# Softmax coefficients sent to the partitions through DRAM, batches in even-first order, and a reordered start, in a two-block conditioned FFN kernel

## The chip, the cores and the metric

One core of a Trainium2 chip runs the whole program. The metric is the device time of one execution in microseconds; the profile is of one execution of the same program.

## The reference, cut to what matters

```python
# block 0: a mixture of 8 channel matrices per batch, then a linear layer with routed LoRA
h = gelu(cond @ W0 + b0); h = gelu(h @ W1 + b1)
att = softmax(h @ W2 + b2)                                  # (64 batches, 8)
agg_w = einsum('bk,koi->boi', att, weight); agg_b = att @ bias_k
z = einsum('boi,bih->boh', agg_w, x) + agg_b[:, :, None]    # channels mixed, per batch
x1 = x + (z @ Wf.T + routed LoRA of z)                      # gates: layer norm, relu, top 2 of 8
# block 1: a grouped convolution over positions, plus ctx = cond @ c_weight.T + fside, then FFN with 8 experts
out = x1 + ffn1(conv(x1) + ctx)
```

x is 64 batches by 64 channels by 1024. All is fp32; each large product is made of three products of rounded parts (high by high, high by low, low by high).

## The kernel before, in words

**Tiles.** The 4096 rows (batch, channel) are 32 tiles of 128 rows, two batches to a tile. Block 0 is phase A, block 1 is phase B. The mixing of channels and the linear layer commute, so phase A first multiplies each tile of x by the linear weights (`main(t, b, k)`, line 1409, in three banks of 384, 416 and 384 columns, 24 matmuls each) and then mixes the channels of that product with a 128x128 block-diagonal matrix of the tile (`mix(t, b, k)`, line 1429, three matmuls). Between the two, ACT rounds the product to a high part (`y_high`, line 746) and DVE writes the low part (`y_low`, line 985). DVE makes the mixing matrix of a tile (`mix_matrix`, line 962) from `attw`, the 8 channel matrices in `consts`, and `attc`, which holds on each partition the 8 softmax coefficients of each tile's batch (even batches on partitions 0 to 63, odd ones on 64 to 127). The bias of the mixture comes in through the column sums of the weights (`column_sums`, line 1379), scaled by `aggc`; `evict` (line 991) adds it and the residual and `route` (line 998) makes the gates.

**The start.** x and the weights of block 0 arrive as plain fp32. SP issues every DMA of the kernel (line 427 on), and the queue lands them in order: the first half of tile 0 of x (`xo`), the weight chunks 0 to 3 (one of the 8 row blocks of bank 0 each), the second half of tile 0 (line 460), chunks 4 to 7, the parameter pack `cbuf` (line 463), tile 1, tile 2, `consts`, chunks 8 and 9 (bank 1), 10 and 11 (bank 2). ACT makes the high part of each chunk (`split_hi`, line 724) and of each tile (`x_high`, line 739), DVE the low part (`split_lo`, line 957; `x_low`, line 979). PE warms up with 8 matmuls on constants and then runs `first_bank` (line 1390): bank 0 of tile 0 with its column sums, one row block after another as they come.

**The conditioning net** is done in between, on PE in five steps (`cond`, line 1357): 0, 1 and 2 are the three layers; 3 transposes `att`, makes the context product, and spreads `att` to the 128 partitions by a matmul of `batch_part` (which partition half a batch belongs to) with `att_m` (att times `batch_tile`, made by DVE at line 1054); 4 is the bias of the mixture. ACT does the GELUs (796, 799) and the exponential (802) with its table load (800), DVE the softmax (1050 to 1052) and the copy of the spread coefficients from PSUM to `attc` (1060). Batches lie in their natural order, so the two batches of a tile are neighbours.

**Order.** Each engine runs a list written out by hand, and semaphores join them; an engine does its list strictly in order. The orders that matter are PE at lines 1447 to 1476, ACT at 779 to 846, DVE at 1025 to 1129, SP at 457 to 493 and POOL at 675 to 694. After the start, PE repeats for each tile of phase A: main bank 1, mix of tile t + 2 bank 0, main bank 2, mix bank 1, main bank 0 of tile t + 3, mix bank 2.

## Time and profile before

| | |
|---|---|
| median of 3 runs | 1265.41 us (1264.41 to 1265.54) |
| the profiled execution's own time | 1265.09 us |
| its span, first to last instruction | 1263.3 us |
| granted TensorE clock, mean over the span | 1.000 |
| PE busy | 1257.2 us |
| DVE busy | 842.7 us |
| ACT busy | 307.3 us |
| POOL busy | 235.2 us |
| DMA moved | 141.55 MB, 112 GB/s in the mean |

The profile has one line for each group of instructions, with the engine, the kernel's line and the operation. PE is the matmul engine, DVE, ACT and POOL are the vector, scalar and general engines, and SP only issues DMAs. A timeline row gives the start from the span's beginning, the duration (of all its instructions together, where it says x2 or more), and in brackets how long the engine had been idle and what released it. Matmuls overlap on PE: the distance from one start to the next is what one costs. The chain of waits follows the work back from the end, at each step to what released it. All times are in microseconds.

### The profile page before, as it was taken

Reading aid. Unit: us, or ns where it says so; the run is one execution under the profiler, and the core shown is the slowest. Engines: PE = TensorE matmul, PEld = TensorE weight load, DVE = VectorE, ACT = ScalarE, POOL = GpSimd, SP = SyncE. Lnnn points to the kernel's source line nnn. Section 1 sums busy time; section 2 is a strip of 40 time slices with the busy share of each in tenths; the row PEclk is TensorE's granted clock in tenths of the full one; section 3 lists DMA queues with packets and bytes.
Section 4 is the critical chain, followed back from the end, with each engine's and each line's share of the span. In section 5 each row is a group of like instructions: output and inputs, shape, how many; then the busy total and the mean of one; then the engine's idle time right before and its main releaser. Section 6 shows DMA issues by size and latency. Waiting matters only on the chain.

```text
span 1263.3 us, 21216 instructions
## 1 busy us (share of the span) xinstructions
PE 1257.2 (100%) x6967; PEld 1165.1 (92%) x6967; DVE 842.7 (67%) x2171; ACT 307.3 (24%) x654; POOL 235.2 (19%) x170
## 2 busy tenths in 40 slices
PE   9999999999999999999999999999999999999998
PEld 8999999999999999888889889888888888988987
DVE  6877866667667667756765765675676576576563
ACT  6323332222223234211121121121121112112110
POOL 1244522232323222011001001001100100100100
PEclk9999999999999999999999999999999999999999
DMA  8355433333334267434223323322423322332310
GB/s 278 129 145 167 146 110 116 128 122 120 114 109 132 91 217 223 123 90 123 71 80 114 88 71 106 106 71 89 122 71 88 116 78 71 113 99 71 98 43 34
DMA packets 84889, 141.55 MB, mean 112 GB/s; under 512 B 6769, under 2 KB 53361, under 8 KB 84849
## 3 DMA queue, kind: packets, MB, share of 16 engines
q1 hardware_dynamic: 84848, 141.04, 36.7%
q8 instruction: 22, 0.36, 0.1%
q14 instruction: 19, 0.15, 0.0%
HBM read 88.57 MB, written 52.45 MB: 112 GB/s over the span
## 4 chain that ended last, share of the span: by engine, by line
PE 97%; DVE 1%; DMA 1%; ACT 0%; SPq 0%; issue 0%
PE ps L1345 30%; PE ps L1347 29%; PE ps L1346 29%; PE ps L1514 5%; PE ps L1516 2%; DMA xo<-in_xt 1%; DVE weights L960 1%; PE ps L1503 0%; PE ps L1480 0%; PE ps L1610 0%; DVE mixs L970 0%; PE ps L1505 0%; DVE mixw L969 0%; SPq L432 0%; ACT L800 0%
## 5 line engine op out<-in xcount | busy, mean ns | idle before, releaser
L1345 PE MATMUL ps<-weights,lhs_h 128*128 128x512 f32 (+3 forms) x1408 | 498.5, 354 | 0.0
L1347 PE MATMUL ps<-weights,lhs_l 128*128 128x512 f32 (+3 forms) x1408 | 489.1, 347 | 0.0
L1346 PE MATMUL ps<-weights,lhs_h 128*128 128x512 f32 (+3 forms) x1408 | 489.0, 347 | 0.0
L1345 PEld LDWEIGHTS ps<-weights,lhs_h 128*128 128x128 f32 x1408 | 264.5, 188 | 23.9 <-issue 0.6
L1347 PEld LDWEIGHTS ps<-weights,lhs_l 128*128 128x128 f32 x1408 | 264.5, 188 | 21.3
L1346 PEld LDWEIGHTS ps<-weights,lhs_h 128*128 128x128 f32 x1408 | 265.2, 188 | 19.8
L715 POOL TENSOR_TENSOR xo<-row,wsum 128x512 f32<-128x512 f32 x60 | 76.8, 1306 | 647.3 <-DMA out_x<-xo 647.3
L1345 PE MATMUL ps<-weights 128*128 128x384 f32 (+1 forms) x376 | 128.8, 343 | 0.0
L1346 PE MATMUL ps<-weights 128*128 128x384 f32 (+1 forms) x376 | 128.1, 341 | 0.0
L1347 PE MATMUL ps<-weights 128*128 128x384 f32 (+1 forms) x376 | 127.9, 340 | 0.0
L1231 DVE TENSOR_TENSOR whole<-ps,whole 64x256 f32<-64x256 f32 x240 | 101.2, 422 | 7.7
L752 ACT ACTIVATE part<-ps 128x384 fp32r<-128x384 f32 (+1 forms) x96 | 47.9, 499 | 239.9 <-PE ps L1347 239.9
L1224 DVE TENSOR_TENSOR whole<-ps,bias_in 64x256 f32<-64x256 f32 x240 | 101.1, 421 | 6.7 <-issue 0.2
L1514 PE MATMUL ps<-conv_hl,part 128*128 128x512 f32 x360 | 99.9, 345 | 0.0
L881 ACT ACTIVATE lhs_h<-whole 128x512 fp32r<-128x512 f32 x64 | 40.5, 633 | 235.6 <-DVE whole L1231 228.3
L988 DVE TENSOR_TENSOR part<-ps,part 128x384 fp32r<-128x384 f32 (+1 forms) x96 | 54.3, 565 | 61.0 <-ACT part L752 59.5
L668 POOL TENSOR_TENSOR row<-row,biased 128x800 f32<-128x800 f32 x31 | 61.2, 1974 | 127.3 <-DMA row<-in_xr 102.3
L1287 DVE TENSOR_TENSOR staging<-ps,mixw 128x256 f32<-128x256 f32 x32 | 13.6, 425 | 96.9 <-PE ps L1347 96.6
L1142 DVE TENSOR_TENSOR row<-ps,row 128x512 f32<-128x512 f32 x60 | 41.5, 692 | 52.8 <-PE ps L1347 52.5
L1514 PEld LDWEIGHTS ps<-conv_hl,part 128*128 128x128 f32 x360 | 67.7, 188 | 6.2
L1315 DVE TENSOR_TENSOR xo<-ps,xo 128x512 f32<-128x512 f32 x64 | 43.2, 692 | 45.3 <-PE ps L1347 45.1
L1347 PEld LDWEIGHTS ps<-weights 128*128 128x128 f32 x376 | 70.7, 188 | 0.4
(201 smaller groups left out, 1622.7 us busy)
## 6 DMA issues: line engine op xcount, KB each, us to landing
row<-spill SPq DMA_DIRECT2D x30, 576.0 KB, 4.2
z<-x_round SPq DMA_DIRECT2D x64, 256.0 KB, 5.1
out_x<-xo SPq DMA_DIRECT2D x31, 512.0 KB, 2.7
xo<-in_xt SPq DMA_DIRECT2D x30, 512.0 KB, 3.5
x_round<-row SPq DMA_DIRECT2D x60, 256.0 KB, 2.1
row<-in_xr SPq DMA_DIRECT2D x31, 400.0 KB, 3.2
spill<-row SPq DMA_DIRECT2D x31, 400.0 KB, 3.8
staging<-in_w SPq DMA_DIRECT2D x9, 832.0 KB, 6.1
```

The source lines that it names most:

```text
L668: pool.tensor_tensor(dst, dst, biased[:, BANK0:OUT0], ALU.add).then_inc(row_ready12, 1)
L715: pool.tensor_tensor(natural[:, PAD * (1 - h):PAD * (1 - h) + J // 2, :], src[:, q].rearrange("p (s i) -> p s i", i=P), b1bc[:, q].rearran ...
L752: act.activation(yh[:, slot, 0:COLS0[k]], ps[:, BY0[slot], 0:COLS0[k]], ACT.Copy).then_inc(y_hi[k], 1)
L988: dve.tensor_tensor(yl[:, slot, 0:n], ps[:, BY0[slot], 0:n], f32(yh[:, slot, 0:n]), ALU.subtract).then_inc(y_lo[k], 1)
L1142: dve.tensor_tensor(base[:, q], ps[:, BP0[h], :], base[:, q], ALU.add).then_inc(x1_ready, 1)
L1224: dve.tensor_tensor(where_to[to, b], parts[q, :, k, 0], add[to, b, :, None, :].to_broadcast([64, 2, J, GC]), ALU.add).then_inc(conv_part, 1)
L1231: dve.tensor_tensor(where_to[to, b], parts[q, :, k, 1], where_to[to, b], ALU.add).then_inc(conv_read, 1)
L1315: dve.tensor_tensor(o, ps[:, BQ[2 + h], :], o, ALU.add).then_inc(y_read, 1)
L1345: pe.matmul(out_ap, lhs[0], rhs[0], start=first, stop=False, skip_group_check=True)
L1346: pe.matmul(out_ap, lhs[0], rhs[1], start=False, stop=False, skip_group_check=True)
L1347: return pe.matmul(out_ap, lhs[1], rhs[0], start=False, stop=last, skip_group_check=True)
L1514: pe.matmul(dst[:, out_k], stationary(t, 0, h, g, w), both[:, rows], start=(w == 1), stop=False, skip_group_check=True)
```

## The change

The spread of the coefficients by DVE and PE is taken out. Instead SP writes `att` to DRAM (`att_rows`) and reads it back twice, once to each half of the partitions. For that the batches are laid out with the 32 even ones first and then the 32 odd ones, which the host does for `cond_128`, and the writing of the context rows (`cond_rows`, now two DMAs) and the bias pick on ACT follow. The parameter pack loses the two tables for the spread and has 594 columns in place of 754. Besides, the start is in another order: the second half of tile 0 is issued by ACT; steps 0 and 1 of the net are inside `first_bank`, step 2 ahead of tile 1, steps 3 and 4 a few row blocks earlier or later; ACT and DVE do the net's work ahead of the split of tile 2; `y_low(0, 0)` comes after the first mixing matrix; and for tile 0 `main(0, 0, 2)` comes ahead of `mix(2, 2, 0)`, with `y_high(0, 2)` and `y_low(0, 2)` earlier.

```diff
# DRAM tensors and the pack
-        cond_rows = nc.dram_tensor("cond_rows", (B, C), F32, kind="Internal").ap()
+        cond_rows = nc.dram_tensor("cond_rows", (TILES, 2, C), F32, kind="Internal").ap()
+        att_rows = nc.dram_tensor("att_rows", (2, TILES * KATT), F32, kind="Internal").ap()
-        CPACK = 754
+        CPACK = 594
# SP
             sp.dma_start(xo[:, 0, 0:512], a["xt"][0:P, 0:512]).then_inc(first_in, 16)
-            for n in range(4):
-                chunk(n)
-            sp.dma_start(xo[:, 0, 512:D], a["xt"][0:P, 512:D]).then_inc(xt_in[0], 16)
-            for n in range(4, 8):
+            for n in range(8):
                 chunk(n)
...
             chunk(8)
             chunk(9)
+            sp.wait_ge(cond_dve, 3)
+            sp.dma_start(att_rows.rearrange("h (t k) -> (h t) k", k=KATT), att).then_inc(att_out, 16)
             sp.wait_ge(x_lo, 3)
             chunk(10)
+            sp.wait_ge(att_out, 16)
+            for h in range(2):
+                sp.dma_start(attc[64 * h:64 * h + 64, :, :].rearrange("p t k -> p (t k)"),
+                             att_rows[h].unsqueeze(0).to_broadcast([C, TILES * KATT])).then_inc(attc_in, 16)
+            chunk(11)
             load_xr0(0, 0)
-            chunk(11)
...
-            sp.wait_ge(cond_dve, 6)
-            sp.dma_start(cond_rows, ctxo).then_inc(cond_out, 16)
+            sp.wait_ge(cond_dve, 5)
+            for h in range(2):
+                sp.dma_start(cond_rows[:, h, :], ctxo[TILES * h:TILES * h + TILES, :]).then_inc(cond_out, 16)
...
# POOL
-            pool.wait_ge(attc_ready, 1)
+            pool.wait_ge(attc_in, 32)
# ACT
-            for n in range(4):
+            for n in range(2):
+                split_hi(n)
+            act.dma_start(xo[:, 0, 512:D], a["xt"][0:P, 512:D]).then_inc(xt_in[0], 16)
+            for n in range(2, 4):
                 split_hi(n)
             act.wait_ge(xt_in[0], 16)
             act.activation(x_hl[0][0][:, 4:8, :], half_x(0, 1), ACT.Copy).then_inc(x_hi, 1)
             for n in range(4, 8):
                 split_hi(n)
-            act.wait_ge(second_in, 16)
-            act.activation(x_hl[1][0][:, 0:4, :], half_x(1, 0), ACT.Copy).then_inc(first_hi, 1)
-            act.wait_ge(xt_in[1], 16)
-            act.activation(x_hl[1][0][:, 4:8, :], half_x(1, 1), ACT.Copy).then_inc(x_hi, 1)
-            y_high(0, 0)
             act.wait_ge(cond_in, 16)
             act.wait_ge(cond_pe, 1)
             act.activation(h1, ps[:, BC[0], 0:B], ACT.Gelu, bias=cb0).then_inc(cond_act, 1)
-            x_high(2, 2, 1)
+            act.wait_ge(second_in, 16)
+            act.activation(x_hl[1][0][:, 0:4, :], half_x(1, 0), ACT.Copy).then_inc(first_hi, 1)
             act.wait_ge(cond_pe, 2)
             act.activation(h2, ps[:, BC[1], 0:B], ACT.Gelu, bias=cb1).then_inc(cond_act, 1)
+            act.wait_ge(xt_in[1], 16)
+            act.activation(x_hl[1][0][:, 4:8, :], half_x(1, 1), ACT.Copy).then_inc(x_hi, 1)
             act.activation(sc[:, 6:7], eps[:, :], ACT.Exp).then_inc(tables, 1)
             act.wait_ge(cond_dve, 2)
             act.activation(ex, lg, ACT.Exp, bias=am[:, 0:1]).then_inc(cond_act, 1)
+            y_high(0, 0)
+            x_high(2, 2, 1)
             column_sums(0)
             split_hi(8)
+            split_hi(9)
             y_high(1, 0)
-            split_hi(9)
-            act.wait_ge(cond_pe, 7)
+            act.wait_ge(cond_pe, 6)
...
# DVE: the softmax's sum and maximum stand between the two halves of tile 1's low part
-            y_low(0, 0)
-            x_low(2, 2)
...
             dve.tensor_scalar(att, ex, am[:, 2:3], None, ALU.mult).then_inc(cond_dve, 1)
-            dve.wait_ge(cond_dve, 3)
-            dve.tensor_tensor(att_m, att[:, None, :].to_broadcast([B, TILES, KATT]),
-                              batch_tile[:, :, None].to_broadcast([B, TILES, KATT]), ALU.mult).then_inc(cond_dve, 1)
+            x_low(2, 2)
             dve.wait_ge(cond_pe, 5)
             dve.tensor_copy(attT, ps[0:KATT, BC[1], 64:64 + B]).then_inc(cond_dve, 1)
             dve.tensor_tensor(ctxo, ps[0:B, BC[1], 128:128 + C], fs_bc, ALU.add).then_inc(cond_dve, 1)
-            dve.wait_ge(cond_pe, 6)
-            dve.tensor_copy(attc[:, :, :].rearrange("p t k -> p (t k)"),
-                            ps[:, BC[0], 128:128 + TILES * KATT]).then_inc(attc_ready, 1)
             split_lo(8)
             split_lo(9)
...
-            dve.wait_ge(attc_ready, 1)
+            dve.wait_ge(attc_in, 32)
             restart(2)
             mix_matrix(0, 0)
+            y_low(0, 0)
             y_low(1, 0)
...
                 if at(t, 0):
+                    y_low(0, 2)
                     mix_matrix(3, 3)
-                    y_low(0, 2)
# PE
                     pe.matmul(ps[0:B, BC[1], 128:128 + C], emb_t, ctx_w, start=True, stop=True).then_inc(cond_pe, 1)
-                    pe.matmul(ps[:, BC[0], 128:128 + TILES * KATT], batch_part, wbuf[0:B, 0:TILES * KATT],
-                              start=True, stop=True).then_inc(cond_pe, 1)
...
                     summed = pe.matmul(sums, ones[:, :], w_lo, start=False, stop=last, skip_group_check=True)
+                    if j in (5, 6):
+                        cond(j - 5)
...
             first_bank()
-            cond(0)
-            main(1, 1, 0, 0, 2)
-            cond(1)
-            main(1, 1, 0, 2, 4)
             cond(2)
-            main(1, 1, 0, 4, 8)
+            main(1, 1, 0, 0, 4)
+            main(1, 1, 0, 4, 6)
             cond(3)
-            main(2, 2, 0, 0, 4)
+            main(1, 1, 0, 6, 8)
+            main(2, 2, 0, 0, 2)
             cond(4)
-            main(2, 2, 0, 4, 8)
+            main(2, 2, 0, 2, 8)
             column_sums(1)
...
                 if at(t, 0):
                     mix(1, 1, 0)
                     column_sums(2)
-                mix(t + 2, (b + 2) % XB, 0)
-                main(t, b, 2)
+                    main(0, 0, 2)
+                    mix(2, 2, 0)
+                else:
+                    mix(t + 2, (b + 2) % XB, 0)
+                    main(t, b, 2)
# ACT, phase A: y_high(0, 2) for tile 0 comes ahead of bias12_of(1)
```

## Rows read from the trace of the kernel before

**Rows 1.** The page: busy time by engine; chain that ended last.

```profile
PE 1257.2 (100%) x6967; PEld 1165.1 (92%) x6967; DVE 842.7 (67%) x2171; ACT 307.3 (24%) x654; POOL 235.2 (19%) x170
...
PE 97%; DVE 1%; DMA 1%; ACT 0%; SPq 0%; issue 0%
```

**Rows 2.** Timeline of PE, first 37 us: start us, us, engine, line, idle before.

```profile
9.53 0.41 PE L1398 MATMUL ps<-weights 128*128 128x384 f32 x1 [0.73 <-ACT weights L737]
...
11.56 0.34 PE L1398 MATMUL ps<-weights 128*128 128x384 f32 x1
...
18.86 0.21 PE L1371 MATMUL ps<-consts,z 64*8 64x64 f32 x1 [0.27 <-DVE whole L1054]
...
19.26 0.70 PE L1373 MATMUL ps<-whole,z 64*128 64x256 f32 x2
19.89 0.45 PE L1345 MATMUL ps<-weights,lhs_h 128*128 128x384 f32 x1
...
27.82 0.34 PE L1345 MATMUL ps<-part,mix_hl 128*128 128x384 f32 x1
...
36.56 0.41 PE L1345 MATMUL ps<-part,mix_hl 128*128 128x384 f32 x1 [0.20 <-DVE row L996]
```

**Rows 3.** Chain of waits, first 62 us: start us, us, what.

```profile
3.09 5.22 DMA xo<-in_xt
...
20.00 0.42 DVE attc L1060
...
22.14 1.89 DVE weights L960
...
35.85 0.57 DVE row L996
```

**Rows 4.** Timeline of ACT, first 22 us.

```profile
4.27 1.02 ACT L737 ACTIVATE weights<-staging 128x384 fp32r<-128x384 f32 x2 [0.21 <-DMA staging<-in_w]
...
15.94 1.28 ACT L800 ACT_TABLE_LOAD   x1
...
18.40 1.59 ACT L737 ACTIVATE weights<-staging 128x1664 fp32r<-128x1664 f32 x1 [0.40 <-DMA staging<-in_w]
...
20.41 1.60 ACT L737 ACTIVATE weights<-staging 128x1664 fp32r<-128x1664 f32 x1
```

**Rows 5.** Timeline of SP: issue of the parameter pack.

```profile
5.48 0.43 SPq L463 DMA_DIRECT2D z<-in_cpack  x1
```

**Rows 6.** DMA issues, first 48 us: KB each, median us to landing.

```profile
staging<-in_w SPq DMA_DIRECT2D x2, 832.0 KB, 8.2
...
z<-in_cpack SPq DMA_DIRECT2D x1, 377.0 KB, 5.9
...
bias_in<-cond_rows SPq DMA_DIRECT2D x2, 64.0 KB, 3.2
cond_rows<-z SPq DMA_DIRECT2D x1, 16.0 KB, 5.0
```

**Rows 7.** Timeline of DVE, first 28 us.

```profile
13.93 0.55 DVE L988 TENSOR_TENSOR part<-ps,part 128x384 fp32r<-128x384 f32 x1
15.75 1.23 DVE L982 TENSOR_TENSOR lhs_l<-xo,lhs_h 128x1024 fp32r<-128x1024 f32 x1 [1.27 <-ACT lhs_h L743]
...
18.04 0.22 DVE L1052 TENSOR_SCALAR z<-whole 64x8 f32<-64x8 f32 x1
...
23.94 0.69 DVE L969 TENSOR_TENSOR mixw<-consts,attc 128x512 f32<-128x512 f32 x1
...
26.33 0.56 DVE L988 TENSOR_TENSOR part<-ps,part 128x384 fp32r<-128x384 f32 x1
```

**Rows 8.** Timeline of DVE, 53 to 60 us: second bank of tile 1.

```profile
58.95 0.56 DVE L988 TENSOR_TENSOR part<-ps,part 128x384 fp32r<-128x384 f32 x1
```

**Rows 9.** Timeline of PE, 60 to 61 us: third mix of tile 1.

```profile
60.70 0.34 PE L1345 MATMUL ps<-part,mix_hl 128*128 128x384 f32 x1
```

**Rows 10.** Line 446, spill store on a quiet queue.

```profile
DMA to landing us min/median/max: 1.8/1.8/1.8
```

More of the change, by code:

```diff
@@ L242, in program @@
         cond_pe, cond_act, cond_dve = sem("cond_pe"), sem("cond_act"), sem("cond_dve")
-        cond_out, attc_ready, aggc_ready = sem("cond_out"), sem("attc_ready"), sem("aggc_ready")
+        cond_out, att_out, attc_in, aggc_ready = sem("cond_out"), sem("att_out"), sem("attc_in"), sem("aggc_ready")
         xt_in, xr0_in, xr12_in, bias_ld = pair("xt_in"), pair("xr0_in"), pair("xr12_in"), pair("bias_ld")
@@ L452, in load_bias @@
             def load_bias(t, u):
-                src = cond_rows.rearrange("b o -> (b o)")[bass.ts(t, P)]
+                src = cond_rows.rearrange("t h o -> (t h o)")[bass.ts(t, P)]
                 sp.dma_start(bias_in[:, u, :], src.unsqueeze(0).to_broadcast([P, P])).then_inc(bias_ld[u], 16)
             sp.dma_start(xo[:, 0, 0:512], a["xt"][0:P, 0:512]).then_inc(first_in, 16)
-            for n in range(4):
-                chunk(n)
-            sp.dma_start(xo[:, 0, 512:D], a["xt"][0:P, 512:D]).then_inc(xt_in[0], 16)
-            for n in range(4, 8):
+            for n in range(8):
                 chunk(n)
@@ L484, in _ @@
             load_xt(5, 1)
-            sp.wait_ge(cond_out, 16)
+            sp.wait_ge(cond_out, 32)
             load_bias(0, 0)
@@ L692, in phase_a @@
                     pool.memset(z[:, :, :], 0.0).then_inc(blank, 1)
-            pool.wait_ge(cond_out, 16)
+            pool.wait_ge(cond_out, 32)
             periods(pool, phase_a)
@@ L802, in _ @@
             act.activation(ex, lg, ACT.Exp, bias=am[:, 0:1]).then_inc(cond_act, 1)
+            y_high(0, 0)
+            x_high(2, 2, 1)
             column_sums(0)
             split_hi(8)
+            split_hi(9)
             y_high(1, 0)
-            split_hi(9)
-            act.wait_ge(cond_pe, 7)
+            act.wait_ge(cond_pe, 6)
             for h in range(2):
                 q = slice(64 * h, 64 * h + 64)
-                pick = ps[q, BC[1], 192:192 + B].rearrange("p (t two) -> p two t", two=2)[:, h, :]
+                pick = ps[q, BC[1], 192:192 + B].rearrange("p (two t) -> p two t", two=2)[:, h, :]
                 act.activation(aggc[q, :], pick, ACT.Copy).then_inc(aggc_ready, 1)
@@ L830, in phase_a @@
                     y_high(t + 2, 0)
+                if at(t, 0):
+                    y_high(0, 2)
                 bias12_of(t + 1)
@@ L834, in phase_a @@
                     root(routed(t))
-                y_high(t, 2)
+                    y_high(t, 2)
                 if before_end(t, XB):
@@ L1047, in _ @@
             dve.tensor_reduce(am[:, 0:1], lg, X, ALU.max, negate=True).then_inc(cond_dve, 1)
+            dve.wait_ge(x_hi, 2)
+            dve.tensor_tensor(x_hl[1][1][:, 4:8, :], half_x(1, 1), f32(x_hl[1][0][:, 4:8, :]),
+                              ALU.subtract).then_inc(x_lo, 1)
             dve.wait_ge(cond_act, 3)
@@ L1369, in cond @@
                     pe.wait_ge(consts_in, 16)
[L1370 removed]
+                    pe.wait_ge(cond_dve, 3)
                     pe.transpose(ps[0:KATT, BC[1], 64:64 + B], att, eye[0:B, 0:B]).then_inc(cond_pe, 1)
                     pe.matmul(ps[0:B, BC[1], 128:128 + C], emb_t, ctx_w, start=True, stop=True).then_inc(cond_pe, 1)
[L1373 to L1374 removed]
                 elif step == 4:
[L1376 removed]
+                    pe.wait_ge(cond_dve, 5)
                     pe.matmul(ps[:, BC[1], 192:192 + B], bias_k, attT, start=True, stop=True).then_inc(cond_pe, 1)
@@ L1642, in laid_out @@
     bias_k[0:KATT] = np.tile(f["L0_cond_bias_k"], (1, 2))
-    b = np.arange(B)[:, None]
-    by_batch = np.zeros((P, KATT + C + P + TILES), np.float32)
+    by_batch = np.zeros((P, KATT + C), np.float32)
     by_batch[0:B, 0:KATT] = f["L0_cond_b2"]
     by_batch[0:B, KATT:KATT + C] = f["fside_S_0"]
-    by_batch[0:B, KATT + C:KATT + C + P] = b % 2 == np.arange(P) // C
-    by_batch[0:B, KATT + C + P:] = b // 2 == np.arange(TILES)
-    a["cpack"] = np.concatenate([f["cond_128"].T, f["L0_cond_W0"], f["L0_cond_W1"], f["L0_cond_W2"],
+    halves = f["cond_128"].reshape(TILES, 2, EMB).transpose(2, 1, 0).reshape(EMB, B)
+    a["cpack"] = np.concatenate([halves, f["L0_cond_W0"], f["L0_cond_W1"], f["L0_cond_W2"],
                                  f["L1_cond_c_weight"].T, f["L0_cond_b0"].reshape(HID, 1),
```

7 lines of the change are left out of this document (removed).

## The prediction

> **What bounds the kernel now.** I read the page first. PE is busy for 1257.2 of 1263.3 us, and 97% of the chain that ended last is PE [rows 1]. So no change outside PE's list is worth anything unless it removes a gap on PE, and the gaps are few. The timeline of PE shows all of them in the first 37 us [rows 2]: 0.73 us before the fifth row block of the first bank (9.53), 0.27 us before the transposition of the coefficients (18.86), 0.20 us before the mix at 36.56. The spread of the coefficients is a full fp32 matmul that PE runs itself: from 19.26 to the next start at 19.89 it costs 0.63 us. Together: 0.73 + 0.27 + 0.20 + 0.63 = 1.83 us, 0.14% of the time. A difference under 0.2% (2.5 us) can't be told from no change here, so even a full success is nearly out of its reach.
>
> Then I read the chain of waits, for what lies behind those gaps [rows 3]. The first is the second half of tile 0: issued at 3.09, it lands 5.22 us later, at 8.31, and ACT and DVE must still split it. From 20.00 to 36.42 the chain runs on DVE alone: the copy of the coefficients, the low parts of chunks 8 and 9, three mixing matrices, evictions, ending with the 0.57 us eviction at 35.85, 0.14 us before PE's mix at 36.56. So in the stretch where the change works there are two clocks, PE's and DVE's, almost equally late. Each part below is costed on both.
>
> **Second half of tile 0 issued by ACT.** It costs ACT nothing that shows: ACT's second weight chunk ends at 5.29 [rows 4], and the chunks keep it waiting then; an issue lasts 0.43 us, as SP's of the pack does [rows 5]. It is issued 2 us later than by SP. No row shows a DMA from ACT's queue. One bound: it stands behind nothing and lands after the 1.8 us of a quiet queue [rows 10], at about 7; the gap of 0.73 us goes. The other: the same 5.22 us from the later issue, 10.5; PE waits 2.2 us more. I take a landing near today's 8.3, since the same bytes must be moved by then. It matters little, because PE now meets the net's step 0 after the sixth row block (today 11.56 [rows 2]) and that needs the parameter pack. The pack is issued at 5.48 and takes 5.9 us, so it lands at 11.4 [rows 5, 6]. It is 80 KB smaller (377 to 297 KB). Two chunks of 832 KB are split 2.01 us apart, at 18.40 and 20.41, where ACT waits for them [rows 4], 414 KB in a us, so 80 KB are 0.19 us. PE passes that point at 11.25 at the best: a gain of 0 to 0.3 us, I take 0.15.
>
> **Steps of the net moved.** The same small matmuls run elsewhere; no cost. Today the softmax result is ready at 18.04 + 0.22 = 18.26 [rows 7], behind the split of tile 2 on ACT and the 1.23 us low part on DVE. Both come after it now, and the exponential's table load (15.94 today [rows 4]) moves up by about 2 us, so it is ready near 16.3. PE asks for it two matmul groups before the end of tile 1's bank, near 17: the 0.27 us gap goes. What is late next is the low part of tile 2: ACT splits it after the softmax, DVE ends at about 18.4 where it ended at 16.98 [rows 7], and PE starts tile 2 at 19.89 - 0.63 - 0.27 - 0.15 = 18.84. A cover of 0.4 us; if it is gone, PE waits what is missing.
>
> **Spread removed.** PE saves 0.63 us [rows 2]. DVE saves the multiply and the 0.42 us copy [rows 3], but gains nothing by it: the low part of chunk 9 starts when ACT has its high part, 20.41 + 1.60 = 22.01 [rows 4], which hangs on the landing. With the smaller pack this is 0.2 us earlier: DVE can start the first mixing matrix at 23.75 in place of 23.94 [rows 7].
>
> **Round trip added.** SP writes the coefficients (issued near 16.4, 8 KB or less in 32-byte rows) behind chunk 9 in its queue. Chunk 9 lands at 20.2, and the write right behind it; by the row of cond_rows, 5.0 us from issue [rows 6], 21.4. Then two reads, 0.45 us each to issue. The nearest row is the broadcast of a context row: 64 KB, the same bytes, 3.2 us, also behind a large load [rows 6]. From 20.4: second read issued at 20.85, landed at 24.05. The lower end is 1.8 us [rows 10], 22.7; the upper is a slow write and the longest transfer of the start, 8.2 us [rows 6]: 21.4 + 0.5 + 8.2 = 30.1. I take 24.0, so DVE starts the mixing matrix 0.1 us later than now. Queued behind SP's new waits are chunk 11 and two rows of x; chunk 11 has 5 us until DVE wants it. POOL's first row work waits on the same reads but starts at the bias anyway.
>
> The Trainium skill (SBUF — State Buffer, The DMA setup-cost knee) speaks against such a small trip: each transfer pays a roughly fixed 2 us whatever its bytes. By that figure the reads would land at 20.85 + 2.0 + 0.15 = 23.0, before DVE is free, and the sum would come out at 1264.8. The trace's quiet store (1.8 us) agrees, its broadcast (3.2 us) doesn't; the sum goes by the trace.
>
> **y_low(0, 0) moved behind the first mixing matrix.** It used to fill idle time of DVE at 13.93; now its 0.55 us (0.5 with overlap) [rows 7] is in the middle of the DVE chain. DVE runs 0.1 + 0.5 = 0.6 us later than today from there on. PE's first mix needs it: 24.0 + (26.33 - 23.94) + 0.5 = 26.9, plus the 0.14 us hand-over, 27.0. PE comes to it at 27.82 - 0.63 - 0.27 - 0.15 = 26.77 [rows 2]. So PE waits 0.25 us there and has gained 0.8.
>
> **main(0, 0, 2) before mix(2, 2, 0).** It puts 24 matmuls of 0.17 us, 4.2 us, between PE and the DVE chain, so the 0.20 us gap at 36.56 goes: gain 1.0. What is late next: DVE's chain isn't faster, it is 0.6 us later, and it goes on without real idle time up to tile 1. The tightest place is the low part of tile 1's third bank, which ends at 58.95 + 0.56 = 59.51 [rows 8], for a mix that PE starts at 60.70 [rows 9]. With DVE 0.6 later plus 0.14: 60.25. PE would be there at 59.7, and waits 0.55 us. Left of the gain: 0.45 us. From tile 2 on DVE follows PE and the rest shifts with it.
>
> **The sum.** Against the profiled execution's 1265.09 us (span 1263.3 and 1.8 around it): 1264.6. The median is 0.3 above it: 1265.41 - 0.45 = 1264.95, I say 1264.9.
>
> **Rivals.**
> *PE's whole gain stays (25%).* If the reads land by 23.7 and DVE has a few tenths of slack that I don't see, the gain is 0.63 + 0.27 + 0.20 + 0.3 = 1.4 us: 1264.0. For it: the quiet store's 1.8 us. Against: the margin at 60.70 is only 1.19 us today. If the half tile came early as well and the pack didn't hold PE, it would be 1.83 us: 1263.6, the ceiling.
> *The half tile comes late (12%).* At 10.5 PE loses 2.2 us at 9.53. It takes up the 0.55 and 0.25 us of waiting for DVE, so 2.2 - 0.8 - 0.45 is about 1 us slower: 1266.4. The Trainium skill (DMA: Bandwidth & Descriptors, Issuing engines are not separate DMA queues) says that DMAs of all issuers run on the same 16 engines and interleave, so that the second issuer saves only issue time; by that rule the half tile shares the bandwidth with the backlog and lands late rather than at 7.
> *The round trip becomes the bound, slower (8%).* DVE's chain starts at the landing of the second read. Each us behind 24.0 first takes the gain of 0.45 and then adds to the time. It is slower by over 2.5 us if the reads land after 27.0; at the upper end, 30.1, it is 1264.9 + 6.1 = 1271.0. For it: DVE and POOL both hang on it, and transfers of the start take up to 8.2 us. Against: those are of 832 KB and these of 64 KB.
> *The change does nothing it is meant to (10%).* The 0.63 us goes, every other gap returns elsewhere, and DVE's 0.6 us stands against it: 1265.4 to 1265.6.
>
> **How the numbers follow.** Forecast 45%, the others as given. The range reaches from the first rival less 0.4 us of scatter (three runs of today differ by 1.1 us) to the late half tile: 1263.6 to 1266.6. Faster by over 0.2% needs more than the ceiling of 1.83 us, and only an unseen gain does it: 3%. Slower by over 0.2%: 8%. Within it: 89%.
>
> **What would show it.** Right: no line 1373, the mix of tile 0 near 27.0 with a short wait on DVE, no gap after the second column sums, a wait of some tenths at tile 1's mixes ended by the low part of y, the matrix of tile 0 started within 0.3 us of 24.0 by the landing of attc. Wrong: a gap over 0.3 us before a matmul of the first bank or before step 0 that is longer than today's 0.73 us; the first mixing matrix after 25; a gap on PE behind 100 us that isn't there today.

## The result and the profile after

The changed kernel takes 1271.57 us (median of 5 runs, 1270.71 to 1272.62) beside 1265.41 us (1264.41 to 1265.92) for the kernel before: 6.16 us or 0.5% slower, ratio 1.0051 with a 95% interval of 1.0037 to 1.0064. The forecast was 1264.9 us and the range ended at 1266.6. The profiled execution of the changed kernel took 1272.62 us, its span 1270.8 us; line numbers are up to 8 higher than before.

The page of the changed kernel, and the waits of PE (us in total, times, longest us), against [rows 1, 2]:

```profile
PE 1259.8 (99%) x6965; PEld 1166.9 (92%) x6965; DVE 839.2 (66%) x2169; ACT 306.7 (24%) x654; POOL 237.1 (19%) x170
```

```profile
PE ps L1398 <- ACT weights L740: 3.7, 1, 3.7
PE ps L1347 <- DVE part L996: 1.6, 2, 1.0
...
PE ps L1347 <- issue: 0.5, 1, 0.5
PE ps L1347 <- DVE row L1004: 0.4, 1, 0.4
```

The gap of 0.73 us before the fifth row block of the first bank is now 3.7 us, and PE waits 2.5 us in all at mixes. PE is also 2.6 us longer busy, though it has less to do. The timeline of PE says where (start us, us, engine, line, form, idle before and releaser):

```profile
12.31 0.66 PE L1398 MATMUL ps<-weights 128*128 128x384 f32 x1 [3.66 <-ACT weights L740]
...
13.08 0.52 PE L1402 MATMUL ps<-weights 128*128 128x384 f32 x1
...
18.62 0.34 PE L1402 MATMUL ps<-weights 128*128 128x384 f32 x1
...
33.28 0.41 PE L1347 MATMUL ps<-part,mix_hl 128*128 128x384 f32 x1 [0.96 <-DVE part L996]
...
38.98 0.42 PE L1347 MATMUL ps<-part,mix_hl 128*128 128x384 f32 x1 [0.41 <-DVE row L1004]
...
57.58 0.41 PE L1347 MATMUL ps<-part,mix_hl 128*128 128x384 f32 x1 [0.53 <-issue]
```

Matmuls of 384 columns last 0.52 us from 12.8 to 18.4 us and follow each other every 0.32 us; from 18.62 they are at 0.34 and 0.175 us again, as before. The windows of the same trace show it as the granted clock (columns: busy time and count of PE, PEld, DVE, ACT, POOL; PEclk; DMA share; GB/s):

```profile
5.00:9.00 4.00, 3.65 (x21) 3.32 (x19) 1.93 (x4) 1.46 (x3) 0.00 (x0) 1.00 0.89 291
9.00:12.30 3.30, 0.00 (x0) 0.03 (x1) 0.52 (x1) 1.18 (x3) 0.00 (x0) 0.90 0.64 248
12.30:18.40 6.10, 6.09 (x20) 6.10 (x21) 2.74 (x6) 2.10 (x6) 0.00 (x0) 0.50 0.77 292
```

PE did nothing from 8.7 to 12.3 us, the clock fell to its lower level (0.50, 1.2 of 2.4 GHz) and stayed there for 6.1 us of work. In the kernel before, the gap was 0.73 us and the clock stayed at 1.00.

What PE waited for is the second half of tile 0 (the half tile from here on), now issued by ACT (timeline of ACT, then the DMA line of that issue):

```profile
4.89 0.41 ACTq L788 DMA_DIRECT2D xo<-in_xt  x1
...
11.12 0.63 ACT L792 ACTIVATE weights<-xo 128x512 fp32r<-128x512 f32 x1 [4.15 <-DMA xo<-in_xt]
```

```profile
DMA to landing us min/median/max: 6.2/6.2/6.2
```

Issued at 4.89, landed 6.2 us later at 11.1; before it was 3.09 and 8.31 [rows 3]. The queue table of the same stretch, 4.5 to 12 us, shows a second queue, q10, with this one transfer in it (144 packets; columns: packets, MB, share of the 16 engines):

```profile
q1 hardware_dynamic: 1190, 1.85, 72.0%
q10 hardware_dynamic: 144, 0.26, 11.3%
```

Its first packet starts at 7.6 us, 2.7 us behind the issue. Of the eight weight chunks, all issued by 4.94, six had landed by then; the last landed at 8.75.

Last, the round trip of the coefficients through DRAM (timeline of DVE at the first mixing matrix, against 23.94 in [rows 7], and the DMA line of the two reads):

```profile
30.07 0.69 DVE L977 TENSOR_TENSOR mixw<-consts,attc 128x512 f32<-128x512 f32 x1 [2.39 <-DMA attc<-att_rows]
```

```profile
DMA to landing us min/median/max: 4.0/4.9/5.7
```

The first mixing matrix is 6.1 us later than before. DVE was idle for the last 2.4 of them, waiting for the coefficients. That wait is in part the start's delay too: the second read was issued at 24.3 us, where run 1 below, with the half tile in time, issues it at 20.3.

In the profiled execution the span grew by 7.5 us. Read off PE: the first gap +2.9 us; four row blocks and two steps of the net at the low clock, 6.9 us from 12.31 to 19.24 where 4.0 us would do, +2.9; waits at the mixes at 33, 39, 58, 63 and 83 us, some 3.2 (from one start to the next, so a little more than the idle times above); less 0.63 for the removed matmul and 0.5 for the two old gaps. That makes 7.9; 0.4 us of it is not resolved. At the mix at 82.72 us PE is 7.5 us behind the same mix of the kernel before (75.21), so all of the growth is in front of it.

### The profile page after: what moved, and what is told of

The parts are those of the page before. It is cut to its first block, busy times and chain, and to the rows that moved or that the text cites. A ratio compares the mean times of both kernels' runs of the same rounds, so it can differ in the third digit from the quotient of the medians.

```text
span 1270.8 us, 21215 instructions
## 1 busy us (share of the span) xinstructions
PE 1259.8 (99%) x6965; PEld 1166.9 (92%) x6965; DVE 839.2 (66%) x2169; ACT 306.7 (24%) x654; POOL 237.1 (19%) x170
## 4 chain that ended last, share of the span: by engine, by line
PE 94%; DVE 3%; DMA 2%; ACT 0%; issue 0%; POOL 0%; SPq 0%; DVEq 0%; POOLq 0%
PE ps L1347 28%; PE ps L1349 28%; PE ps L1348 28%; PE ps L1517 5%; PE ps L1519 2%; DMA xo<-in_xt 0%; DMA attc<-att_rows 0%; PE ps L1506 0%; DMA spill<-row 0%; DVE part L996 0%; DVE mix_hl L981 0%; PE ps L1483 0%; PE ps L1613 0%; DVE mixs L978 0%; DVE weights L968 0%
```

## The experiments

Each time is the median of its runs, beside the kernel before on the same chip at the same time: 1264.99 us for experiments 1 to 4, 1265.17 for 5 to 8, 1265.07 for 9 to 12 and 1265.22 for 13 to 15. The difference to that is what is compared. The brackets give the ratio and its 95% interval, which is 2.3 to 4.2 us wide, so that two experiments whose intervals overlap are not told apart with certainty. Edits are against the changed kernel where nothing else is said.

**1. Half tile back on SP, in its old place.**

```diff
-            for n in range(8):
-                chunk(n)
+            for n in range(4):
+                chunk(n)
+            sp.dma_start(xo[:, 0, 512:D], a["xt"][0:P, 512:D]).then_inc(xt_in[0], 16)
+            for n in range(4, 8):
+                chunk(n)
...
-            act.dma_start(xo[:, 0, 512:D], a["xt"][0:P, 512:D]).then_inc(xt_in[0], 16)
```

> Changed kernel with the second half of tile 0 issued by SP again, between weight chunks 3 and 4; all else as changed. Theory A (two causes: the half tile, and the round trip): the gap of 4 us before the fifth row block goes back to about 0.7 and the clock stays at its high level, but the coefficients land at 26 to 27, since in the changed kernel the reads took 5.7 us behind chunk 10; the first mixing matrix then starts 2 to 3 us later than in the kernel before, and the time is 1266 to 1268. Theory B (the half tile alone costs, the round trip is hidden as predicted): coefficients in by 24.1, time 1264.5 to 1265.3.

Measured 1268.13 us, +3.14 (ratio 1.0027, interval 1.0017 to 1.0038), where the changed kernel had +6.16. The half tile lands at 8.14, PE's gap is 0.6 us. Half of the loss is gone and half stays. The second read landed at 24.3, near the 24.0 that the prediction had taken, but DVE was there at 23.2 and waited 1.3 us. Theory A holds in kind; the time is 0.13 us above its range, and the landing it named (26 to 27) was too late. The half that stays is the round trip and the reordering together, as run 4 shows. The wait, and the DMA line of the reads:

```profile
  DVE mixw L977: 1.3, 1
...
DMA to landing us min/median/max: 2.7/3.3/4.0
```

**2. The same edit the other way: kernel before, only the half tile moved to ACT.**

```diff
-            sp.dma_start(xo[:, 0, 512:D], a["xt"][0:P, 512:D]).then_inc(xt_in[0], 16)
+            # in ACT's list, behind split_hi(1)
+            act.dma_start(xo[:, 0, 512:D], a["xt"][0:P, 512:D]).then_inc(xt_in[0], 16)
```

> Kernel before with one thing changed: the second half of tile 0 issued by ACT after its second weight chunk. Theory A and B both: the half tile lands at about 11, PE waits some 4 us at the fifth row block, its granted clock falls to the low level for some microseconds after it, and PE loses in all 5 to 6 us against before, less what of it was DVE's wait anyway: 1269.5 to 1271.5. Rival C (the lateness in the changed kernel comes from the other moves, the ACT issue alone is harmless): 1265 to 1266.

1269.13 us, +4.14 (1.0031, 1.0020 to 1.0041), 0.4 us below the range expected. The transfer took 6.9 us and landed at 11.9, and the same two things follow, a gap of 3.5 us and a fallen clock:

```profile
PE ps L1398 <- ACT weights L734: 3.5, 1, 3.5
```

```profile
9.00:13.00 4.00, 0.60 (x4) 0.28 (x2) 0.39 (x1) 1.06 (x3) 0.00 (x0) 1.00 0.53 199
13.00:17.40 4.40, 4.27 (x15) 4.05 (x16) 3.38 (x7) 2.27 (x5) 0.00 (x0) 0.61 0.70 234
```

So this one line costs 4.1 us by itself. Rival C falls. In two of the nine runs the mean clock was 1.000, and they are the two shortest, 1266.65 and 1267.41; the seven at 0.998 or 0.999 took 1268.70 to 1271.77.

**3. Matmul spread back, half tile still on ACT.**

```diff
+            dve.tensor_tensor(att_m, att[:, None, :].to_broadcast([B, TILES, KATT]),
+                              batch_tile[:, :, None].to_broadcast([B, TILES, KATT]), ALU.mult).then_inc(cond_dve, 1)
...
+            dve.tensor_copy(attc[:, :, :].rearrange("p t k -> p (t k)"),
+                            ps[:, BC[0], 128:128 + TILES * KATT]).then_inc(attc_in, 1)
...
+                    pe.matmul(ps[:, BC[0], 128:128 + TILES * KATT], batch_part, wbuf[0:B, 0:TILES * KATT],
+                              start=True, stop=True).then_inc(cond_pe, 1)
...
-            sp.dma_start(att_rows.rearrange("h (t k) -> (h t) k", k=KATT), att).then_inc(att_out, 16)
```

> Changed kernel with the coefficients spread by the matmul and the two DVE operations again (batches still even ones first), ACT still issues the half tile. Theory A (the round trip costs beside the half tile): the DVE wait of 2.4 us for the coefficients and the gaps of 0.6, 0.7, 0.2 and 0.8 us on PE at 39, 58, 63 and 83 us go, 0.6 us of matmul comes back: 1269.5 to 1270.5. Theory B (round trip hidden): 1272.0 to 1272.4, the 0.63 us of the matmul on top.

1270.03 us, +5.04 (1.0040, 1.0027 to 1.0052), 1.1 less than the changed kernel's +6.16. That is in theory A's range, but of the four gaps that it named only the one at 39 us is gone, with the one at 33; those at 56, 61 and 81 stay (0.9, 0.2 and 0.9 us), so they are not the round trip's.

**4. Both undone: the reordered start alone** (edits 1 and 3 together).

> Both undone: SP issues the half tile in its old place and the matmul spreads the coefficients; what is left is the reordered start alone. Theory A and B: the gaps at 18.9 and 36.6 of the kernel before are gone and nothing new is there, 1264.6 to 1265.3. Rival D (the reordering itself costs, as by y_low(0, 0) in the middle of DVE's chain): 1265.6 to 1267.

1266.95 us, +1.96 (1.0013, 1.0003 to 1.0022). Theory A and B both fall here, rival D holds: the order itself costs. Timelines of PE, DVE and POOL:

```profile
33.17 0.41 PE L1348 MATMUL ps<-part,mix_hl 128*128 128x384 f32 x1 [0.96 <-DVE row L999]
```

```profile
26.10 1.02 DVE L991 TENSOR_TENSOR part<-ps,part 128x384 fp32r<-128x384 f32 x2
27.04 2.29 DVE L963 TENSOR_TENSOR weights<-xo,weights 128x1536 fp32r<-128x1536 f32 x1
29.25 1.50 DVE L972 TENSOR_TENSOR mixw<-consts,attc 128x512 f32<-128x512 f32 x1
...
32.46 0.56 DVE L999 TENSOR_TENSOR row<-ps,row 128x384 f32<-128x384 f32 x1
```

```profile
26.70 1.02 POOL L659 TENSOR_TENSOR row<-row,biased 128x384 f32<-128x384 f32 x1 [24.78 <-DMA row<-in_xr]
28.53 1.68 POOL L659 TENSOR_TENSOR row<-row,biased 128x384 f32<-128x384 f32 x1 [0.81 <-ACT biased L760]
```

The mix of tile 1 waits for the eviction of tile 0 (line 999 here, 996 before), because both use the same PSUM bank. The eviction is the end of DVE's chain: chunk 10, the second mixing matrix, then it. That chain has the moved low part of y in it (26.10, two of them), which adds 0.47 us, and two of its operations are stretched, 2.29 and 1.50 us in place of 1.75 and 0.68, which adds 1.36.

The POOL rows tell why. The chunk began at 27.04 with 0.68 us of POOL's first row work left and took 0.54 us longer; the mixing product began at 29.25 with 0.95 us of the second left and took 0.82 longer. In the kernel before, the products at 23.94 and 28.47 began just ahead of POOL's work at 24.02 and 28.67 and took 0.69 and 0.68 us. Two moves bring them together here: POOL's first piece waits for the row of x, which SP now loads behind chunk 11, and the low part of y makes DVE later. An estimate from these rows: without it the chunk would begin at 26.57 and the product at 28.24, ahead of POOL both times (26.70 and 28.53), and the eviction would end at 31.2, a microsecond before PE comes at 32.2. So a move of 0.5 us costs DVE up to 1.8.

**5. Filler matmuls in the wait for the half tile.**

```diff
+                    if j == 4:
+                        keep_warm(16)
                     if j % 4 == 0:
                         pe.wait_ge(*((first_hi, 1) if first else (x_hi, 1)))
```

> Changed kernel with 16 matmuls of 512 columns on constants ahead of the fifth row block of the first bank, in the time in which PE waits for the half tile (they write a bank that is not in use yet). In the changed kernel 20 matmuls after the wait ran 0.147 us longer each, with the granted clock at the low level, 3 us in all. Theory A (the clock's fall is a cost of its own): the half tile still lands at about 11, the matmuls behind it come at 0.174 us, PE reaches tile 1 about 2.5 us earlier, and since DVE's chain hangs on PE and the landings there, 1.5 to 2.5 us of it stay: 1269 to 1270. Rival E (DVE or the landings bound what comes after, the clock costs nothing): 1271 to 1271.8.

1272.48 us, +7.31 (1.0060, 1.0043 to 1.0076) in 4 runs, outside both ranges. The clock was at 1.00 behind the filler, but that ended at 13.4, a microsecond behind the time at which PE resumed in the changed kernel (12.31). In this profile the first four row blocks ended 1.2 us later too; the matmuls of the first one took 0.52 us each. It is no measure of the clock's cost; run 13 repeats it.

**6. Half tile on SP, but behind all eight chunks.**

```diff
             for n in range(8):
                 chunk(n)
+            sp.dma_start(xo[:, 0, 512:D], a["xt"][0:P, 512:D]).then_inc(xt_in[0], 16)
...
-            act.dma_start(xo[:, 0, 512:D], a["xt"][0:P, 512:D]).then_inc(xt_in[0], 16)
```

> Changed kernel with the half tile issued by SP, but behind all eight weight chunks, at about the time at which ACT issued it. Theory F (place in the queue is what matters, the issuer is not): it lands at 10.5 to 11.2 as with ACT, the gap is about 3.5 us and the time 1270.5 to 1271.7. Theory R (ACT's own ring is late to start and slow to end, first packet 2.7 us after the issue): it lands at 9.2 to 9.5, half a microsecond behind chunk 7, the gap is 1.5 to 2 us, and the time is 1269 to 1270.3.

1270.26 us, +5.09 (1.0042, 1.0025 to 1.0059) in 4 runs. Issued at 4.99, landed at 9.84, between the two theories; gap and time are in the range of theory R. The gap is 2.0 us and the clock falls for a shorter time (granted 0.87 from 11 to 13 us, 0.50 to 15, 0.78 to 17). ACT's timeline:

```profile
9.86 0.63 ACT L790 ACTIVATE weights<-xo 128x512 fp32r<-128x512 f32 x1 [2.65 <-DMA xo<-in_xt]
```

So of the 2.8 us that the half tile is later in the changed kernel's profile, some 1.5 are its place behind the chunks. The 1.3 us left can't be put down to ACT's queue as such: in run 14, the changed kernel again, the half tile was issued by ACT at 4.47 and landed at 9.87. The intervals of this run and of the changed kernel overlap.

**7. Half tile by ACT, as its very first instruction.**

```diff
+            act.dma_start(xo[:, 0, 512:D], a["xt"][0:P, 512:D]).then_inc(xt_in[0], 16)
             act.wait_ge(zeroed, 2)
...
-            act.dma_start(xo[:, 0, 512:D], a["xt"][0:P, 512:D]).then_inc(xt_in[0], 16)
```

> Changed kernel with the half tile issued by ACT as its very first instruction, 4 us earlier. Theory G (the late issue is the cost): it lands by 6, the gap before the fifth row block goes altogether, chunks 0 to 3 land up to 0.6 us later, and what is left is the cost of the round trip and of the reordering: 1267 to 1268.5, as with the half tile in SP's old place. Theory R (ACT's ring is slow whatever the time of issue): lands after 8, gap of 1 us or more, over 1268.5.

1267.09 us, +1.92 (1.0016, 1.0006 to 1.0025). It lands at 4.2, 3.4 us from issue, and PE has no gap there at all:

```profile
DMA to landing us min/median/max: 3.4/3.4/3.4
```

Theory G holds, and theory R falls for a queue that is asked early. The late issue is the cost, 4.2 us of the changed kernel's 6.2.

**8. Both undone, and the low part of y of tile 0 early again** (against run 4).

```diff
+            y_low(0, 0)
             x_low(2, 2)
...
             mix_matrix(0, 0)
-            y_low(0, 0)
```

> Kernel with both parts undone (half tile by SP, matmul spread) and in addition the low part of y of tile 0 taken out of the middle of DVE's chain, to ahead of the low part of tile 2. That kernel without this edit measured 1266.95. Theory H (0.5 us more in DVE's chain costs that much, and PE's gaps at 33, 52 and 77 shrink by it): 1266.2 to 1266.6. Rival I (the chain is late for other reasons, POOL's row work now beside DVE's splits and the spill behind the bias loads): 1266.8 to 1267.2.

1266.00 us, +0.83 (1.0008, 0.9999 to 1.0018), where run 4 had +1.96. The runs spread widely, 1263.73 to 1267.80; the profiled one is the 1263.73, and in it the waits of PE have only the one ahead of the warm-up, so no gap over 0.15 us behind it:

```profile
PE ps L1356 <- DVE weights L1028: 1.6, 1, 1.6
```

```profile
24.89 1.75 DVE L963 TENSOR_TENSOR weights<-xo,weights 128x1536 fp32r<-128x1536 f32 x1
26.55 0.69 DVE L972 TENSOR_TENSOR mixw<-consts,attc 128x512 f32<-128x512 f32 x1
...
28.94 0.56 DVE L999 TENSOR_TENSOR row<-ps,row 128x384 f32<-128x384 f32 x1
```

The chunk and the mixing product are at 1.75 and 0.69 us and the eviction starts 3.5 us earlier than in run 4. Not all of that is the edit: chunk 9 landed 1.7 us earlier in this execution (18.55, in run 4's 20.24). The step from run 4 is 1.1 us, below the range of theory H, and the two intervals overlap, so its sign is likely and its size is not shown. A profile of the fastest of ten runs shows what is possible, 1.4 us under the profiled execution of the kernel before, not what is usual.

**9. Run 8 with SP's first row load ahead of chunk 11.**

```diff
             chunk(10)
-            chunk(11)
             load_xr0(0, 0)
+            chunk(11)
```

> The last kernel (half tile by SP, matmul spread, y_low early; 1266.0) with the first row load of x put ahead of chunk 11 in SP's list again. There POOL's first row work waited for that load until 26.7 and then ran beside DVE's chunk and mixing work, two of whose operations took 2.29 and 1.50 us in place of 1.75 and 0.68. Theory J (that collision is part of what the reordering costs): the operations are back at 1.75 and 0.68, 1264.6 to 1265.4. Rival K (the rest comes from elsewhere, such as the net's steps inside the first bank, which meet the parameter pack's landing): no change, 1265.7 to 1266.4.

1265.96 us, +0.89 (1.0007, 0.9998 to 1.0016), in the range of rival K: no change. The chunk's low part is at 1.75 us, but the mixing product at 27.6 is at 1.52 still, because it began 0.15 us behind POOL's second row work (27.46). The collision moved and did not go. Here the second mix does not wait all the same: the low part of y is out of the chain, and the eviction ends at 31.4. The one wait of a mix is at 75.10, 0.7 us. That the rest of the cost comes from the net's steps, as rival K has it, is not shown.

**10. Kernel before, tile 0's order alone** (ACT's `y_high(0, 2)` moves with it).

```diff
+                    main(0, 0, 2)
+                    mix(2, 2, 0)
+                else:
+                    mix(t + 2, (b + 2) % XB, 0)
+                    main(t, b, 2)
...
+                    y_low(0, 2)
                     mix_matrix(3, 3)
-                    y_low(0, 2)
```

> Kernel before with the order of tile 0 alone changed: main(0, 0, 2) ahead of mix(2, 2, 0), with y_high(0, 2) and y_low(0, 2) earlier. Theory L (as in the prediction): the 0.20 us gap at 36.6 goes and nothing new comes, 1264.7 to 1265.0 beside 1265.1 for the kernel before. Rival M (y_low(0, 2) ahead of the fourth mixing matrix and the shift open a gap at 52 us as in the changed kernel): 1265.3 to 1266.2.

1265.93 us, +0.86 (1.0003, 0.9994 to 1.0012), in the range of rival M but within the noise by its interval. The 0.20 us gap at 36.6 is gone, and a wait of 0.8 us at 75 us is there in its place:

```profile
PE ps L1347 <- DVE part L990: 0.8, 1, 0.8
```

Another 0.7 us is lost late, at 501 us. No gain shows; whether it loses can't be told.

**11. Kernel before, the round trip alone**, even batches first, the write and the two reads where the changed kernel has them; the multiply, the matmul and the copy of the spread are out.

```diff
+            sp.wait_ge(cond_dve, 3)
+            sp.dma_start(att_rows.rearrange("h (t k) -> (h t) k", k=KATT), att).then_inc(att_out, 16)
             sp.wait_ge(x_lo, 3)
             chunk(10)
+            sp.wait_ge(att_out, 16)
+            for h in range(2):
+                sp.dma_start(attc[64 * h:64 * h + 64, :, :].rearrange("p t k -> p (t k)"),
+                             att_rows[h].unsqueeze(0).to_broadcast([C, TILES * KATT])).then_inc(attc_in, 16)
```

> Kernel before with the round trip alone in place of the matmul spread, even batches first. Theory A (the round trip costs more than it saves): the second read lands at 24.5 to 27, DVE idles 1 to 2.5 us before the first mixing matrix and PE gets gaps of 1 to 2 us in all behind 27 us, less the 0.63 us matmul: 1265.6 to 1267. Theory B (hidden, as predicted): 1264.4 to 1265.1.

1266.72 us, +1.65 (1.0013, 1.0004 to 1.0022). The second read lands at 24.27 and DVE waits 1.5 us for it. PE waits at three mixes, 0.75 us at 27.20 and twice for the eviction (waits of PE):

```profile
PE ps L1345 <- DVE row L1002: 2.1, 2, 1.5
```

Theory A holds: the trip costs more than the 0.63 us it saves.

**12. Run 9 with the half tile by ACT first.**

```diff
+            act.dma_start(xo[:, 0, 512:D], a["xt"][0:P, 512:D]).then_inc(xt_in[0], 16)
             act.wait_ge(zeroed, 2)
...
-            sp.dma_start(xo[:, 0, 512:D], a["xt"][0:P, 512:D]).then_inc(xt_in[0], 16)
```

> The kernel of this call's first run with the half tile issued by ACT as its first instruction in place of SP. If the half tile was the only bad part of the reordered start, the gap of 0.3 to 0.7 us before the fifth row block goes too and this is the fastest: 1264.0 to 1265.0. Rival K (the net's steps in the first bank wait for the pack, whatever comes before): no better than that kernel, 1264.8 to 1266.2.

1264.94 us, -0.13 (0.9998, 0.9989 to 1.0007): the best of these kernels and not shown to be faster than the one before. The time lies in both ranges expected, so it does not decide between them; the profile does for one point: PE meets step 0 of the net at 11.17, the pack landed at 9.74, and there is no wait. The profile has 0.3 us of waits in the first bank and 0.4 us late, at 499 us.

**13. Twelve fillers in place of 16, and 14. the changed kernel again**, timed together.

```diff
-                        keep_warm(16)
+                        keep_warm(12)
```

> Changed kernel with 12 filler matmuls in the wait for the half tile, in place of the 16 of the earlier run, which outlasted the wait by about a microsecond (PE resumed at 13.41 us, in the changed kernel at 12.31). Theory A (the clock's fall costs time of its own): PE resumes near 12.4 at the high clock, reaches the first mix at 30.5 to 31 where the changed kernel came at 33.28, and 1 to 2.5 us of it show: 1269 to 1270.5. Rival E (DVE's chain behind the landings takes all of it up again): within 0.5 us of the changed kernel run beside it, 1271 to 1272.

> The changed kernel itself, as the measure for the other two of this call. 1271.57 before; expected 1271.0 to 1272.0 by every theory.

1270.78 us (1270.02 to 1271.41) and 1271.90 us (1270.43 to 1273.38), +5.56 and +6.68. With the filler the clock is at 1.00 throughout and PE resumes at 12.52:

```profile
9.00:12.30 3.30, 3.30 (x16) 2.46 (x14) 0.31 (x1) 0.97 (x3) 0.00 (x0) 1.00 0.57 215
12.30:18.40 6.10, 5.94 (x34) 5.39 (x34) 3.86 (x9) 4.51 (x11) 0.00 (x0) 1.00 0.69 217
```

Run 13 is just above theory A's range and 1.1 us below run 14, so neither theory holds as stated. By the medians the clock's fall is worth about 1.1 us of the time, not the 2.9 that PE shows. The mean clock of each run says more. All five with the filler are at 1.000. Of run 14 four are at 0.998 or 0.999, with 1271.51 to 1273.38 us, all above the filler's highest; against them the filler gains 1.6 us. The fifth is the profiled one, 1270.43: there chunk 1 landed at 4.44 us in place of 4.86, ACT, which waits for it, issued the half tile at 4.47 in place of 4.89, it landed at 9.87 in place of 11.10, the gap was 1.7 us and the clock didn't fall. So part of the scatter of the changed kernel is whether the half tile lands in time to spare the clock. PE still waited 2.0 us at the first mix (30.48) in that execution, so DVE's chain takes much of such a gain.

**15. Chunk 10 behind the reads.**

```diff
-            sp.wait_ge(x_lo, 3)
-            chunk(10)
             sp.wait_ge(att_out, 16)
             for h in range(2):
                 sp.dma_start(attc[64 * h:64 * h + 64, :, :].rearrange("p t k -> p (t k)"),
                              att_rows[h].unsqueeze(0).to_broadcast([C, TILES * KATT])).then_inc(attc_in, 16)
+            sp.wait_ge(x_lo, 3)
+            chunk(10)
```

> Changed kernel with chunk 10 (768 KB) issued by SP behind the two coefficient reads in place of ahead of them. Theory N (the reads were slow because they stood behind chunk 10): issue to landing of the second read falls from 5.7 to 2 to 3 us, the coefficients are in by 27, DVE's wait of 2.4 us for them goes, chunk 10 lands 0.5 to 1 us later, and the time falls by 1 to 2.4 us beside the changed kernel: 1269.2 to 1270.6. Rival O (64 reads of one DRAM row are slow in themselves): still 4 us or more from issue to landing, no gain, 1271 to 1272.

1271.97 us (1269.48 to 1272.13), +6.75. The reads fell from 5.7 to 3.9 us at the most and DVE's wait for them from 2.4 to 0.3:

```profile
  DVE mixw L977: 0.3, 1
...
DMA to landing us min/median/max: 2.6/3.3/3.9
```

The median didn't follow: chunk 10 lands at 31.2 in place of 29.4, chunk 11 at 33.9 in place of 31.6, in a profile whose half tile landed 0.6 us later than the changed kernel's. But the five runs are of two kinds, and the median falls in the slower. Two are at a mean clock of 1.000 and took 1269.48 and 1269.66, in theory N's range; three are at 0.997 to 0.999 and took 1271.97 to 1272.13. Compared with their like in run 14 that is some 0.9 and 0.3 us less, too few runs to call a gain. Part of the slow read is the large load in front of it, as theory N has it. Rival O isn't settled: the second read still took 3.9 us with none in front, but chunk 10 was issued 0.6 us behind it.

## Why the prediction was wrong

**What bounds the kernel** held: PE is the chain, and all of the loss is gaps and slow matmuls in PE's first 85 us.

**The half tile** is the step that failed, and the largest part of the miss: "I take a landing near today's 8.3, since the same bytes must be moved by then. It matters little". It landed at 11.1 in the profile, 2.8 us later, beyond even the bound of 10.5. Two things were wrong in it. That the same bytes must be moved says nothing of which come first: chunks 4 to 7, which PE wants later, were in front, and the second queue's first packet came 2.7 us behind its issue. Run 6 gives the place about 1.5 us of the lateness, run 7 shows that an early issue from the same queue lands early (4.2) and leaves no gap. And the rival for it priced a gap of 2.2 us and left out what follows a gap: the granted clock at 0.50 for 6.1 us. The rival stood at 12% and 1 us slower; alone the edit costs 4.1 us (run 2), undoing it gives 3.0 (run 1). The pack landed where it was predicted (11.33, predicted 11.2 to 11.4), but as PE's next limit it did not show: no run has a wait for it, and in run 12 it is in at 9.74, 1.4 us before PE comes to step 0.

The Trainium skill (DMA: Bandwidth & Descriptors, Issuing engines are not separate DMA queues) was cited for that rival: a second issuer saves issue time only. Here the trace agrees: the half tile shared the engines with the pack and tile 1, and landed 0.2 us ahead of the pack.

**The round trip** was right in the landing and wrong in what it cost. With the half tile in time the coefficients were ready to be sent by 16.05 in run 1 (predicted 16.3), and the second read lands at 24.3 (runs 1 and 11; predicted 24.0). But DVE was ready at 22.9 to 23.2, not at 23.75, so the wait is 1.3 to 1.5 us. By itself the trip costs 1.65 us (run 11) where the sum had a gain. In the changed kernel the reads took 4.0 and 5.7 us and the second landed at 29.9. The rival for a late landing gives 1271.0 us for 30.1, which is near the 1271.57 measured. That is luck: it took a slow write and a slow transfer as the cause, and what came was a late issue, behind the late half tile.

**y_low(0, 0)** was sized at 0.5 us on DVE, absorbed to 0.25 at the first mix. In run 4 the first mix (26.92) does not wait at all, and the second does, 0.96 us at 33.17. The sum left out two things: that the second mix waits for the first eviction, at the far end of that chain, and POOL. The 0.47 us put two DVE operations behind the start of POOL's row work, which made them 1.36 us longer. The prediction says of this work only that it "starts at the bias anyway"; in run 4 it started at the landing of the row of x, behind chunk 11. Taking y_low out brought 1.1 us between the medians of runs 4 and 8, with overlapping intervals; in run 8's profile both operations have their old length.

**main(0, 0, 2) first** removed the 0.20 us gap, as said, and no gain in time shows (run 10). The tightest place was named at the third mix of tile 1, with a wait of 0.55 us. That mix waits in none of these profiles (67.44 in the changed kernel). The waits are one mix earlier and later: at tile 3's bank 0 (57.58 in the changed kernel, 52.04 in run 4), a little at tile 1's bank 1 (62.59), and at tile 2's bank 2 (82.72, and 75.15 in run 10), beyond "from tile 2 on DVE follows PE".

**The 0.63 and 0.27 us** were right: line 1373's matmul and the wait before the transposition are gone in the profile after, and the losses cover what they are worth. The signs of being wrong that the prediction named came as well: a gap in the first bank longer than 0.73 us, and a first mixing matrix after 25.

**The ceiling** of 1.83 us held: no kernel here is faster than the one before beyond its interval. The side of the losses was not bounded in the same way. The parts alone cost 4.14 (half tile), 1.65 (round trip) and 1.96 (order), 7.75 in sum against 6.16 to 6.68 together. That they overlap because they delay the same chain is likely but not shown; the difference is within the intervals.

What stays open: why runs of the reordered start with the half tile in time spread so far (1265.01 to 1268.27 in run 4, at a clock of 1.000 in all ten; the kernel before stays within 1.2 to 2.5), where the order of DVE's and POOL's starts, a few tenths apart and worth up to 0.8 us each, is a likely cause that one profile for each kernel can't show; how much of the clock's fall reaches the end; and single gaps of 0.1 to 1.0 us on PE between 478 and 508 us in the profiles of runs 3, 5, 10, 12 and 14, which the profiles of the kernel before and of the changed kernel's first runs don't have.

## What to carry to other kernels

When everything that can be won is 2 us of a start whose engines and queue are all nearly late, price each move by what it can lose: a transfer that the bounding engine is already waiting for must not be issued later or behind transfers that are wanted later. A load on a second queue can help if it is issued first (some 1 us between the medians of runs 9 and 12, not clear of the noise), and an idle stretch on PE has to be counted with the slow matmuls that may follow it. For every operation put into a co-critical chain, follow the chain to all its waiters, the release of a PSUM bank among them, and look at what another engine does beside it: half a microsecond can change which of the two starts first.

## What the runs showed of the hardware

Gaps of 3.5 to 3.8 us on PE (changed kernel, runs 2, 3 and 15) were followed by matmuls at the granted clock 0.50 for some microseconds: 384 columns every 0.32 us in place of 0.175. Gaps of 0.3 to 1.0 us were not. In between it went both ways: after run 6's 2.0 us gap at 11.05 the clock was at 0.50 for a shorter time; after run 14's gaps of 1.7 us at 11.09 and 2.0 us at 30.48, and run 11's of 1.45 us at 38.22, it stayed at 1.00.

A 256 KB load was on the way for 3.4 us when it was ACT's first issue, and for 5.4, 6.2 and 6.9 us when issued at 4.5, 4.9 and 5.1 us (runs 14, changed kernel, 2), with its first packet 2.7 us late in the changed kernel. The 2 KB write of coefficients in 32-byte rows landed in 1.7 us behind chunks that had landed, and in 3.8 us in run 1, right behind chunk 9. The two 64 KB reads of one DRAM row each took 2.6 to 5.7 us.

A low part of a chunk or a mixing product on DVE that began while POOL was in its row work took longer by all but some 0.13 us of what was left of POOL's operation: 2.29 in place of 1.75 us with 0.68 left (run 4, 27.04), 1.50 in place of 0.68 with 0.95 left (run 4, 29.25), 1.52 with 0.97 left (run 9, 27.61). Begun just ahead of POOL's operation, the same product took 0.68 or 0.69 us (kernel before at 23.94 and 28.47, run 8 at 26.55, run 10 at 27.96). In all these profiles reductions (0.69 us) and the operations that read PSUM (0.55 or 0.56 us) kept their time beside POOL.
